# Two of eight low halves per quad move from VectorE to GpSimd in a two-layer convolution kernel

## The reference

```python
x = x + conv9x9(group_norm(x), w0) + bias      # zero padding of 4
x = x + conv5x5(group_norm(x), w1)             # reflected padding of 2
```

## Time and profile before

| | |
|---|---|
| median of 3 runs | 257.42 us (257.38 to 258.62) |
| the profiled execution's own time | 258.03 us |
| its span, first to last instruction | 255.9 us |
| busy: TensorE, VectorE, ScalarE, GpSimd | 226.4, 220.2, 156.6, 0.9 us |
| granted TensorE clock, mean of the span | 0.978 of full speed |

### The profile page before, as it was taken

How to read it: one execution, slowest core, us unless ns; L and a number is a source line. 1 busy time by engine, 2 the same in 40 slices (tenths; PEclk the granted TensorE clock), 3 DMA queues, 4 the chain that set the end, 5 groups by cost and what they waited for, 6 DMA issues and landing times.

```text
span 255.9 us, 4019 instructions
## 1 busy us (share of the span) xinstructions
PE 226.4 (88%) x1388; PEld 138.8 (54%) x1388; DVE 220.2 (86%) x473; ACT 156.6 (61%) x320; POOL 0.9 (0%) x10
## 2 busy tenths in 40 slices
PE   0071967999899999999799999999999999999994
PEld 0071444666466656555466666555666665655552
DVE  4979999987999989999989879999997087978943
ACT  4977158998959947799666583466447001758310
POOL 1000000000000000000000000000000000000000
PEclk9997697999999999999999999999999999999999
DMA  6960001423002500003500200035020000630122
GB/s 181 415 266 0 0 0 42 100 49 92 0 0 63 138 2 3 1 0 100 190 6 0 95 0 0 3 99 193 6 92 0 3 0 0 177 118 21 75 92 92
DMA packets 7780, 17.37 MB, mean 68 GB/s; under 512 B 3280, under 2 KB 3920, under 8 KB 7760
## 3 DMA queue, kind: packets, MB, share of 16 engines
q1 hardware_dynamic: 6944, 16.83, 20.2%
q10 hardware_dynamic: 816, 0.29, 0.4%
HBM read 5.51 MB, written 4.72 MB: 40 GB/s over the span
## 4 chain that ended last, share of the span: by engine, by line
PE 50%; DVE 30%; ACT 10%; issue 5%; DMA 2%; SPq 0%; DVEq 0%; ACTq 0%
PE banks L1227 27%; PE banks L1242 23%; DVE X L679 5%; ACT junk L950 5%; DVE lo L646 2%; DMA X<-in_x 2%; ACT P L968 2%; DVE wl L505 2%; DVE arg L493 1%; ACT hi L991 1%; DVE wl L531 1%; DVE partU L601 1%; DVE partU L594 1%; DVE g2t L511 1%; DVE s L611 1%
## 5 line engine op out<-in xcount | busy, mean ns | idle before, releaser
L1227 PE MATMUL banks<-hi,wh 128*128 128x368 f16 (+4 forms) x288 | 53.2, 332 | 11.5 <-ACT wh L1023 5.1
L1227 PE MATMUL banks<-lo,wh 128*128 128x368 f16 (+4 forms) x288 | 51.3, 324 | 0.0
L1227 PE MATMUL banks<-hi,wl 128*128 128x368 f16 (+4 forms) x288 | 50.3, 320 | 0.0
L1227 PEld LDWEIGHTS banks<-hi,wh 128*128 128x128 f16 x288 | 28.4, 102 | 30.5 <-issue 9.3
L950 ACT ACTIVATE junk<-X 128x576 bf16<-128x576 f32 x60 | 40.9, 682 | 3.2 <-DMA X<-in_x 0.7
L1227 PEld LDWEIGHTS banks<-lo,wh 128*128 128x128 f16 x288 | 28.6, 99 | 18.0 <-issue 1.0
L1227 PEld LDWEIGHTS banks<-hi,wl 128*128 128x128 f16 x288 | 28.1, 98 | 17.0
L1242 PE MATMUL banks<-lo,wh 128*128 128x384 f16 x160 | 31.6, 328 | 0.0
L1242 PE MATMUL banks<-hi,wh 128*128 128x384 f16 x160 | 31.6, 328 | 0.0
L1242 PE MATMUL banks<-hi,wl 128*128 128x384 f16 x160 | 31.6, 328 | 0.0
L991 ACT CAST hi<-s 128x384 f16<-128x384 f32 x32 | 15.3, 510 | 23.5 <-DVE s L611 10.4
(11 more groups left out here) (120 smaller groups left out, 232.9 us busy)
## 6 DMA issues: line engine op xcount, KB each, us to landing
X<-in_x SPq DMA_DIRECT2D x8, 576.0 KB, 9.6
out<-X SPq DMA_DIRECT2D x7, 576.0 KB, 3.4
work<-X SPq DMA_DIRECT2D x8, 432.0 KB, 3.8
work<-X SPq DMA_DIRECT2D x8, 144.0 KB, 3.6
wh<-work SPq DMA_DIRECT2D x12, 72.0 KB, 2.1
wl<-work SPq DMA_DIRECT2D x12, 72.0 KB, 2.0
stage<-in_w SPq DMA_DIRECT2D x1, 640.0 KB, 7.8
work<-X SPq DMA_DIRECT2D x32, 12.0 KB, 2.3
```

The costliest lines, as they stand in the source:

```text
L1227: ins = nc.tensor.matmul(dst[:, :, o0:o1], wbuf[1][:, i, t * P:(t + 1) * P], src[:, :, o0 + dx:o1 + dx], start=(part == 0 and at == 0), st ...
```

## The change

A constant `OWN_LOW = 6` is new: VectorE makes the low halves of k = 0 to 5 of quads 1, 2 and 3, and GpSimd those of k = 6 and 7 (streams 5 and 6), six subtractions in all, each behind its high half. Quad 0 stays as it was. GpSimd's are counted by a semaphore of their own, `pool_low`; `lo_done` counts the rest, and `lows1(qd)` is its count before quad qd. TensorE waits for the one or the other. Before VectorE overwrites the streams with those of the next quad (`stream1`, `ends1`) it waits for both counts of the quad before. No DMA and no matmul changes.

```diff
--- before.py
+++ after.py
@@ -93,8 +93,15 @@
 WARMING = 13
 ZDMA = 6
 
+OWN_LOW = 6
+
 BANKS1 = (0, 1, 2, 3, 4, 0, 1, 5)
 BANKS2 = ((6, 2, 3, 0), (1, 4, 5, 6)) * 3 + ((2, 3, 0, 1), (4, 5, 6, 2))
+
+
+def lows1(qd):
+
+    return 8 + OWN_LOW * (qd - 1) if qd > 0 else 0
 
 
 def table_constants():
@@ -213,6 +220,7 @@
         turned = {(i, part): sem(f"turned{i}{part}") for i in MIRROR for part in ("h", "l")}
         hi_done = {c: sem(f"hi{c}_done") for c in (1, 2)}
         lo_done = {c: sem(f"lo{c}_done") for c in (1, 2)}
+        pool_low = sem("pool_low")
         conv_mm = {c: sem(f"conv{c}_mm") for c in (1, 2)}
         m_read = {c: sem(f"m_read{c}") for c in (1, 2)}
         mid_done = {c: sem(f"mid{c}_done") for c in (1, 2)}
@@ -605,7 +613,7 @@
 
             def stream1(qd, i):
                 wait(dve, hi_done[1], 8 * qd)
-                wait(dve, lo_done[1], 8 * qd)
+                lows_done1(qd)
                 if i in (1, 2):
                     parts_at(qd, 2)
                     ins = tt(s1_at(i), even("U"), odd("U"), ALU.add if i == 1 else ALU.subtract)
@@ -726,6 +734,11 @@
                 wide1(qd)
                 for i in (3, 4, 5, 6):
                     stream1(qd, i)
+
+            def lows_done1(qd):
+
+                wait(dve, lo_done[1], lows1(qd))
+                wait(dve, pool_low, (8 - OWN_LOW) * (qd - 1))
 
             def low_halves(c, n, ks):
                 for k in ks:
@@ -807,7 +820,7 @@
                 wide1(1)
                 for i in (3, 4, 5, 6):
                     stream1(1, i)
-                low_halves(1, 1, range(4, 8))
+                low_halves(1, 1, range(4, OWN_LOW))
 
             def second_quad():
                 layer2_sums()
@@ -837,7 +850,7 @@
                 rows2(1)
                 small_stats(1, 3)
                 streams1_wide(2)
-                low_halves(1, 2, range(4, 8))
+                low_halves(1, 2, range(4, OWN_LOW))
                 end2(1, 2)
                 end2(1, 3)
 
@@ -877,7 +890,7 @@
                 middle2(3)
                 rows2(3)
                 streams1_wide(3)
-                low_halves(1, 3, range(4, 8))
+                low_halves(1, 3, range(4, OWN_LOW))
                 end2(3, 2)
                 end2(3, 3)
                 small_stats(2, 2)
@@ -1180,6 +1193,13 @@
             nc.gpsimd.memset(ones[:, :], 1.0 / P).then_inc(ones_set, 1)
 
 
+            for qd in range(1, NQ):
+                for k in range(OWN_LOW, 8):
+                    i = S1[k]
+                    pool.wait_ge(hi_done[1], 8 * qd + k + 1)
+                    nc.gpsimd.tensor_tensor(lo[1][:, i, :], s32_1[:, i, :], hi[1][:, i, :], ALU.subtract).then_inc(pool_low, 1)
+
+
         @block.tensor
         def _(pe):
             def bank7(key):
@@ -1213,8 +1233,10 @@
                 for part, (wbuf, xbuf) in enumerate(((wh, hi), (wh, lo), (wl, hi))):
                     if part == 0:
                         pe.wait_ge(hi_done[1], 8 * qd + k + 1)
-                    if part == 1:
-                        pe.wait_ge(lo_done[1], 8 * qd + k + 1)
+                    if part == 1 and qd > 0 and k >= OWN_LOW:
+                        pe.wait_ge(pool_low, (8 - OWN_LOW) * (qd - 1) + k - OWN_LOW + 1)
+                    elif part == 1:
+                        pe.wait_ge(lo_done[1], lows1(qd) + k + 1)
                     for at, t in enumerate(taps):
                         if qd == 0 and part != 1 and at == 0 and i in MIRROR:
                             pe.wait_ge(turned[i, "h" if part == 0 else "l"], 16 * RB)
```

## The result

The changed kernel takes 258.08 us in the median of 20 runs (257.89 to 258.61), against 257.46 us for the kernel before (20 runs, 257.28 to 258.62). The ratio is 1.0024, with a 95% interval of 1.0017 to 1.0031: 0.4 to 0.8 us more. That is inside the forecast range and inside the 0.5% that was named as no change, but with this many runs it is a loss and not a tie: the interval is 0.07% to either side, much finer than the 0.5% that the prediction allowed itself. The measured median lies a little nearer to rival B (258.5) than to the forecast (257.5).

The account below looks back on a forecast made before the run. VectorE was taken to bound the kernel only through TensorE's start on quad 2. On the profiled run 258.03 - 0.94 + 1.03 = 258.1 us, or 257.5 on the median; range 256.3 to 258.8.

Parts of the forecast that it names:

- rival B: Both quad 1 subtractions hold VectorE ahead of the `g2t` sums, 2 x 1.03 us lost; 258.5 us, chance 0.22.
- The place: Before quad 2: VectorE sets the end only through TensorE's start there, at 124.81 us, with 1.88 us lost.
- The removal, -0.94 us: Quad 1: VectorE gives up two low halves of 0.47 us each, and the whole 0.94 us reaches the end.
- Rival C: GpSimd starts late or slowly and TensorE waits at 95.92; 257.0 us for 10 us delay; chance 0.06 with anything else.
- GpSimd's length, 1.03 us, ends 0.41 and 1.23: Each GpSimd subtraction: three streams on one fixed part take 1.03 us; one stream 0.41, three separate passes 1.23.
- The cover of 8 us for k = 6: Quad 1: GpSimd's low halves are there by 87.3, TensorE asks for k = 6's at 95.92, so no wait.
- The unseen term, +1.03 us: Quad 1: GpSimd's SBUF reads hold VectorE for one of two subtractions, 1.03 us, between nothing and 2.06.
- Rival A: No hold at all: quad 1's full 0.94 us arrives, giving 256.5 us; chance 0.32.
- its variant: Quad 1: GpSimd waits its turn until 87.9 and loses no one's time; counted within the 256.5 us case.
- What would show it: Signs in the changed profile: `g2t` starting at 85.3, its sums' lengths, and TensorE's quad 2 start at 123.9, 124.9 or 125.9.
- If both do, B: Quad 1: both `g2t` sums taking about 2.3 us or starting 1 us late would mean rival B.
- One of its signs of being wrong: Anywhere: a low half from GpSimd taking over 2 us would make the prediction wrong.

Follow-up runs that it names:

- e1_skip: Changed kernel without the GpSimd loop and the waits for it, so no engine makes the six low halves; 256.57 us against 257.53, ratio 0.9967.
- e3_extra: Kernel before, plus two GpSimd subtractions in quad 1 that go into a spare buffer; ratio 1.0055, 1.41 us over 257.53.
- e5_copy: Kernel before, plus two GpSimd copies in quad 1 (one stream read, not two) into a spare buffer; ratio 1.0024.
- e10_one: Changed kernel with both low halves of a quad made in one GpSimd instruction of 768 elements; ratio 1.0020.

## Why the prediction was right in the time and wrong in one term

- **The place.** That only TensorE's start on quad 2 counts, and VectorE sets it: right. Quads 2 and 3 alone are worth nothing (1.0003), and in all eleven changed kernels the difference of the stage is the difference of the time, within the intervals.
- **The removal, -0.94 us:** right; -0.93 in the run that makes nothing instead. Rival C's sum, though, takes 0.5 us for the vanished wait for `wclamp`, where its row shows 0.26. The runs bear 0.5 out: TensorE's limit before quad 2 is 120.98 + 0.825 - 83.71 = 38.10 us into the stage in e1_skip and 38.59 before. Why it is more than the wait was not looked into.
- **GpSimd's length, 1.03 us, ends 0.41 and 1.23:** measured 0.92 with no one in its way. Three streams on one fixed part, sized from the memsets, was 12% too long. The Trainium skill, GPSIMD Engine Reference, section "Elementwise — side-by-side cycle accounting", gave an estimated 0.9 us; the trace agrees with it at 0.92.
- **The cover of 8 us for k = 6, and no wait for `lo` at TensorE:** right. Rival C did not happen.
- **The unseen term, +1.03 us: this step failed.** It says that "one of the two subtractions falls across `g2t` and the other can fall beside the PSUM-fed ones": both fell across `g2t`, as rival B said. But each held VectorE by 0.73 us and not by a whole 1.03: the subtraction is shorter than that, 0.92 us, and 0.19 us of it hold no one. So the term is 1.46 us, the sum +0.52 and not +0.09, and B, with the number of holds right and their length too long, had 1.12 us, which is 0.6 too much. Two errors, one hold for two and 1.03 for 0.73, partly cancelled, and that is luck: the forecast of 257.5 us was 0.6 below the measured 258.08, and rival B's 258.5 was 0.4 above it. The range held because it had been drawn out to B; the path of the forecast, one hold beside a free subtraction, did not happen.
- **Rival A** is refuted by the changed kernel itself (the `g2t` sums, 4.15 us for 2.69) and by e3_extra, e5_copy and e10_one; its variant, that GpSimd "waits its turn until 87.9", by the timeline. The two engines took turns: neither kept the other out for more than one instruction.
- **What would show it.** "If both do, B" was the right reading. One of its signs of being wrong came true: a low half from GpSimd took over 2 us, 2.08 in quad 1. The forecast's sum had VectorE wait for GpSimd and never GpSimd for VectorE; the second subtraction stood behind a `g2t` sum. It cost no time, since TensorE asks for that low half more than 8 us later. The absolute times given there (`g2t` at 85.3, TensorE at 124.9 or 125.9) were of less use, since the profiled execution ran 0.5 us ahead from the first load on. A stage's length should have been named.

## What to carry to other kernels

A GpSimd elementwise instruction that reads SBUF is not free beside VectorE. In this kernel it held a VectorE instruction with two SBUF inputs for most of its own length, 0.73 us for 384 + 384 elements, where the same work costs VectorE itself 0.47; so moving it there without a look at its neighbours lost, though GpSimd was idle. Started by a semaphore beside instructions with an input from PSUM, the same two subtractions were free (0.36% faster than before), and with three more of layer 2 the gain was 0.9%. And when an effect is smaller than the jitter of the first load, compare the length of the stage that the change touches, not spans or start times.

## What was not expected of the hardware

- A VectorE `tensor_scalar` over 128x4 float32 in SBUF, with one tensor input and a pointer scalar, was held by a GpSimd subtraction (0.67 us for 0.22); the same operation over 128x1 was not (204 ns each), nor were its neighbours over 128x1 (0.15 us). Why the form makes the difference was not tried further.
- The two engines took turns at instruction boundaries, whichever was first: GpSimd's 768-element subtraction waited 0.74 us for one `g2t` sum and then held the next for about 1.47 us.
- The length of the hold follows what is read: 0.31 us for each copy (384 float32), 0.72 or 0.73 for each subtraction (384 float32 and 384 float16), 1.47 for 768 and 768, nothing for a memset of 1.03 us. Alone these take 0.53, 0.92 and 1.75 us, so the hold is the instruction less 0.2 to 0.3 us each time. Whether its length goes by the elements read or by the time of an instruction that reads can't be told apart from these runs.
